# Two edits of VectorE's instruction order in a fused attention and expert layer: the block choice ahead of the key marks, two expert passes ahead of the selected normalization

## The reference

```python
s_b = einsum('bhtd,bhnd->bhtn', q, k_c) / scale
logits_c = where(c_ok, s_b, NEG)
_, top_idx = top_k(logits_c, 4)                       # the block choice
...
logits_s = where(allowed, einsum('bhtd,bhtnd->bhtn', q, k_s) / scale, NEG)
out_s = einsum('bhtn,bhtnd->bhtd', softmax(logits_s), v_s)
...
sc, ix = top_k(sim, 8)                                # key scores
scores, pk = top_k(all_sc, 8)                         # pair sums
w = silu(einsum('btd,bthkd->bthk', h, de)) * softmax(scores)
experts_states = einsum('bthk,bthkd->btd', w, ue)
```

## Time and profile before

| | |
|---|---|
| median of 3 runs | 1492.84 us (1491.62 to 1496.29) |
| profiled execution | 1490.08 us |
| its span, first to last instruction | 1488.3 us |
| mean granted TensorE clock | 0.981 |
| busy | PE 1399.5, PEld 1041.1, DVE 1148.8, ACT 927.1, POOL 946.8 us |
| the 1152.1 us from 252.1 on (30 units) | PE 1128.6, DVE 985.2, ACT 759.6, POOL 792.2 us busy, clock 1.00 |

### The profile page before, as it was taken

The page is one execution under the profiler, slowest core; times in us unless marked ns, Lnnn a source line. Parts: engine busy times, 40 slices in busy tenths (PEclk is TensorE's granted clock), DMA queues, the critical chain, the costliest instruction groups (busy, mean ns, idle before and its releaser), DMA issues. The chain is left out here.

```text
span 1488.3 us, 43616 instructions
## 1 busy us (share of the span) xinstructions
PE 1399.5 (94%) x14864; PEld 1041.1 (70%) x14960; DVE 1148.8 (77%) x4512; ACT 927.1 (62%) x1684; POOL 946.8 (64%) x877
## 2 busy tenths in 40 slices
PE   6899569999999999999999999999999999999978
PEld 4566437777777777777777777777777777777757
DVE  5444378888888888888888888888888888888712
ACT  3776436666666666666666666666666666666641
POOL 4655357777777766666666666666676666666720
PEclk8999969999999999999999999999999999999989
DMA  6556842211112222222212222122222222222027
GB/s 187 202 192 213 269 82 54 52 44 48 46 47 51 52 52 52 52 50 47 47 47 47 50 52 47 48 52 52 52 52 52 52 52 52 66 52 53 9 83 250
DMA packets 217149, 113.76 MB, mean 76 GB/s; under 512 B 128872, under 2 KB 211224, under 8 KB 217112
## 3 DMA queue, kind: packets, MB, share of 16 engines
q1 hardware_dynamic: 216304, 112.88, 27.9%
q10 hardware_dynamic: 808, 0.42, 0.2%
HBM read 73.08 MB, written 40.16 MB: 76 GB/s over the span
## 5 line engine op out<-in xcount | busy, mean ns | idle before, releaser
L1394 DVE TENSOR_REDUCE bmax<-q_bank 128x32 f32<-128x512 f32 (+3 forms) x512 | 221.2, 487 | 34.4 <-PE q_bank L1635 34.2
L1149 POOL TENSOR_TENSOR sumxy<-xy 128x1024 f32<-128x1024 f32 x128 | 246.1, 1942 | 0.0
L1241 ACT ACTIVATE pts<-k_bank 128x512 f32<-128x512 f32 (+2 forms) x384 | 177.4, 490 | 42.2 <-PE k_bank L1670 41.4
L1115 POOL TENSOR_TENSOR pad<-pad 128x1 f32<-128x1 f32 x32 | 6.2, 193 | 287.4 <-DVE top L1413 287.4
L1495 DVE SCALAR_TENSOR_TENSOR mw<-sumxy,c,ex 128x1024 f32<-128x1024 f32 x128 | 162.0, 1287 | 13.4 <-ACT ex L1259 9.6
L1617 PE MATMUL f_bank<-xt,wfu 128*128 128x128 f32 x1024 | 162.4, 281 | 0.0
L1635 PE MATMUL q_bank<-ko,qo 96*128 96x512 bf16 (+3 forms) x512 | 142.6, 306 | 16.9 <-DVE bmax L1394 16.7
L1175 POOL TENSOR_TENSOR cw<-cw,mw 128x1024 f32<-128x1024 f32 x64 | 150.9, 2358 | 11.5 <-ACT mw L1265 8.9
L1617 PE MATMUL f_bank<-xt,wfg 128*128 128x128 f32 x1024 | 150.3, 279 | 0.0
L1617 PEld LDWEIGHTS f_bank<-xt,wfu 128*128 128x128 f32 x1024 | 139.4, 191 | 11.5
L1318 ACT ACTIVATE oT<-k_bank 128x512 f32<-128x512 f32 x64 | 38.2, 597 | 173.8 <-PE k_bank L1685 129.3
(11 more groups left out here) (211 smaller groups left out, 3307.8 us busy)
## 6 DMA issues: line engine op xcount, KB each, us to landing
qo<-s_qs SPq DMA_DIRECT2D x192, 64.0 KB, 2.2
ko<-s_ks SPq DMA_DIRECT2D x186, 64.0 KB, 2.2
s_qs<-parts SPq DMA_DIRECT2D x8, 768.0 KB, 4.7
s_ks<-parts SPq DMA_DIRECT2D x8, 768.0 KB, 6.3
s_v<-vo SPq DMA_DIRECT2D x8, 544.0 KB, 3.0
vv<-s_v SPq DMA_DIRECT2D x32, 136.0 KB, 2.3
vw<-s_v SPq DMA_DIRECT2D x64, 68.0 KB, 2.5
xin<-in_L_attn_x_dram SPq DMA_DIRECT2D x8, 512.0 KB, 7.1
```

Source lines behind the costliest of these rows:

```text
L1149: done("sum_done", g_.tensor_tensor(sumxy[:, h, :, :], xy[:, 0, h, 0:XK, None].broadcast_to([P, XK, KEYS]), xy[:, 1, h, None, :].broadcast ...
L1241: last = s.activation(pts[:, h, OFFS[j]:OFFS[j] + n], bank[:, 0:n], ACT.Exp)
L1394: last = v.tensor_reduce(bmax[:, i, h, 0:n], Q.bank(job)[:, o:o + n * BLK].rearrange("p (n j) -> p n j", j=BLK), AX.X, ALU.max)
```

## The change

In VectorE's step `unselected(n, now=t)` moves from behind head 2's block maxima to a place ahead of `key_marks(n)`. `expert(., 0)` and `expert(., 1)` move from the start of the step of their own unit to the end of the step ahead, behind `pair_sums` and ahead of `normalize(t, 0)`; `lead` gets them for unit 0. No instruction is added or dropped, and no other engine's program changes.

```diff
@@ lead(n), VectorE
                     local_scores(n)
                     selected_max(n)
                     cn.end()
+                    expert(n, 0)
+                    expert(n, 1)
 
                 def step(t):
                     n = None if t.tail else t.next()
                     cf.start(t)
-                    expert(t, 0)
-                    expert(t, 1)
                     expert_silu(t, 0)
                     expert(t, 2)
                     expert_silu(t, 1)
@@ step(t)
                     expert_sum(t)
                     if n:
+                        unselected(n, now=t)
                         key_marks(n)
                     gate(t, 1)
                     if n:
                         for part in range(3):
                             block_max(n, 2, part)
                     if n:
-                        unselected(n, now=t)
                         best_pairs(n)
                     up(t, 1)
```

## The result

The changed kernel takes 1512.61 us (median of 6 runs, 1509.89 to 1514.29), the kernel before 1492.08 us (6 runs). The ratio is 1.0132, with a 95% interval of 1.0116 to 1.0148. The prediction was 1507 us with a range of 1500 to 1519.

What follows compares the result with a forecast made beforehand. TensorE, busy 94% of the span, and its waits for VectorE were taken as the bound. 0.46 us in 31 steps gave 14.3 us, the passes 0: 1490.1 + 14.3 = 1504.4 profiled, 1507 us median with 2.8 added; range 1500 to 1519.

Steps and rivals of the forecast that it cites:

- TensorE and VectorE in step between the loads of head 1 and head 2: From 730.2 to 734.5 in a unit: VectorE is the later engine, TensorE waits microsecond for microsecond for anything added.
- The choice costs 0.43 us in its new place: Block choice straight behind expert_sum: 0.43 us instead of 1.97, as GpSimd's third sum has ended by then.
- The chained wait costs 0.04 us, 0.46 in all: Marks wait for the choice's end: 0.04 us, making 0.46 us a unit with the choice, 14.3 us over 31 steps.
- its high end: Pause behind the choice of 0.15 us, as at 737.48, instead of 0.04: 0.58 us a unit.
- the nearer row: Rows of the same form with GpSimd idle, the lead's and the marks' link, taken as grounds for 0.46 us.
- the marks' link: Chained wait between the marks' last replace and xy, 0.04 us, taken as the model for the choice's.
- The lead's row: The choice's instruction in the lead, where GpSimd stands idle: 0.43 us, taken for its new place.
- The freed time at the old place is worth nothing: Behind head 2's maxima VectorE gains some 2.1 us, which becomes idle time because TensorE itself is late next.
- The passes meet `shift_s` and `at` and take turns with them: Tail: pass 0 waits for shift_s, ends 750.67; at follows to 751.40; pass 1 ends 752.48.
- cover of 0.6 us: Tail: VectorE stands ready for pass 2 at 754.7, which is due at 755.32.
- The earlier front gains nothing, pass 2 hangs on ScalarE: Front of a unit: 2.48 us without passes turn idle, pass 2 stays at 755.32 behind ScalarE's exponential; gain 0.
- The lead costs nothing: Lead, which gets the passes for unit 0: the prediction's sum has no term for it.

Runs made afterwards that it cites:

- e1: From the kernel before, only the block choice moves ahead of the key marks; the expert passes stay. 1511.09 us, ratio 1.0129.
- e3: From the kernel before, only the choice moves, with the key marks' own wait for the best keys put ahead of it. 1506.95 us, ratio 1.0091.
- e5: As e1, with the choice's instruction issued a second time ahead of it into a tile that nothing reads. 1519.31 us, ratio 1.0183.
- e2: From the kernel before, only the two expert passes move into the tail; the block choice stays. 1495.01 us, ratio 1.0011.
- e7: e6 with the two expert passes moved into the tail, as in the changed kernel. 1480.95 us, ratio 0.9925.
- e8: As e2, but in the lead the passes wait until GpSimd has finished pc. 1492.84 us, ratio 1.0005.
- e6: From the kernel before, second half of the strike-outs behind head 2's maxima, block choice behind the second up product. 1477.05 us, ratio 0.9902.
- e4: From the kernel before, second half of the strike-outs moves behind head 2's maxima, straight ahead of the block choice. 1487.93 us, ratio 0.9975.

## Why the prediction was right, point by point

- *TensorE and VectorE in step between the loads of head 1 and head 2; what is put there is paid in full.* Right. e1 (0.58 us a unit), e3 (0.10 less) and e5 (0.33 more) move in the unit's length what they move on VectorE, to 0.02 us.
- *The choice costs 0.43 us in its new place, with no GpSimd instruction against it.* Right: 0.41 us. GpSimd's small instruction starts 0.31 us behind the running sum (744.83), before 0.32, and doesn't get ahead.
- *The chained wait costs 0.04 us, 0.46 in all.* This term was mis-sized. It is 0.15 us, which the prediction had seen at 737.48 and kept as its high end: 0.58 us a unit (its own terms give 0.57), which is what was measured. The reason for the nearer row was wrong: the marks' link is followed by no second wait, the choice's is, and in a loop that wait's value is computed in a register. e3 and the written-out unit show it. With 31 units this accounts for 3.7 of the 5.6 us by which 1507 was too low. The lead's row, with constant waits, was no guide to the loop.
- *The freed time at the old place is worth nothing.* Right: VectorE's waits for query products went from 34.2 to 99.2 us.
- *The passes meet `shift_s` and `at` and take turns with them; pass 0 ends 1.08 us behind `shift_s`; cover of 0.6 us.* Right to 0.15 us for the turns: `shift_s` ended at 763.50, pass 0 at 764.57, `at` at 765.16, pass 1 at 766.24. The cover was larger, 0.91 us: the result ended 3.91 us behind `shift_s` (767.41), worked out were 4.24. Pass 2 was also due 0.11 us later against `shift_s`, and 0.13 us of the gain went into the wait for the tanh. The same tanh makes one reading of the prediction wrong: without the meeting its rows give a cover of 0.95 us, not of 2, because the silu half waits for 753.69 in any case. These rows agree with the rule that the prediction cites from the Trainium skill, "SBUF — State Buffer", section "Who interferes with whom", on a VectorE instruction with two SBUF inputs.
- *The earlier front gains nothing, pass 2 hangs on ScalarE.* Right: e2's units, and e7's where TensorE no longer waits for VectorE.
- *The lead costs nothing.* This was not priced, and the same rule would have told it. In the lead pass 0 gets its turn ahead of `pc`, and TensorE starts on `pc` 1.0 us later against the start of the unit (e8 undoes it). It is at most 1 us, and in e2 the first unit is longer by 0.1.

The sum: 0.58 us in each of the 31 units that prepare another one is 18.0 us of the 20.5 between the medians; the other 2.5 us are not placed. The profiled executions differ by 24.2 us: 17.4 in units 1 to 30, 2.3 us in the first unit, 4.2 us before it, 0.3 behind.

The 2.3 us of the first unit can be told apart. The choice is 0.56 of them, as e1's first unit has 42.60 us. The rest fits a second stretch at half clock that only this execution has. In all ten profiles the granted TensorE clock is 0.50 when the first unit begins and 1.00 from 1.7 to 4.4 us later on. In that of the changed kernel it then goes back once more, to 0.50 from 220.69 to 224.10. In the 3.41 us at 1.00 ahead of that TensorE was busy for 1.34 us, as it waited 2.07 us for `pc`; in e2 and e7 a wait of 1.75 us had no such fall behind it. The two stretches (us, PE, PEld, DVE, ACT and POOL busy, granted clock, DMA share, GB/s):

```profile
217.28:220.69 3.41, 1.34 (x6) 0.69 (x6) 3.38 (x5) 1.08 (x3) 3.33 (x4) 1.00 0.01 2
220.69:224.10 3.41, 3.41 (x7) 1.36 (x6) 1.93 (x3) 2.00 (x4) 0.93 (x1) 0.50 0.00 0
```

TensorE is busy throughout the second, and 3.41 us at half the clock are worth at most 1.7 us (an estimate).

The 4.2 us before the first unit are not the passes' doing. The first unit began at 214.1 to 215.4 us in the profiles of the three kernels with the passes in the lead and no wait ahead (changed, e2, e7), and at 210.1 to 212.4 in the seven others. But TensorE's first product of the lead, which lies ahead of everything that was moved, already starts at 191.4 to 192.7 us in those three and at 187.7 to 189.7 in the others. The time from there to the first unit is 22.1 to 22.7 us in all ten. Why the stages ahead of it ended later in these three is open; no run here separates it from scatter. It would account for e7's 3.9 and e2's 2.5 us.

## What to carry to other kernels

Before moving an instruction, find the two waits of the bound engine between which its new place lies: there it is paid in full, elsewhere it may be free, and 0.4 us without a wait can cost more than 2 us spent waiting where nobody is late. An engine's idle time is a place for work only up to the next thing that it must deliver: e6 moved 1.4 us of the same engine's work across the last such point and gained nearly what both waits were worth (0.50 of 0.57 us a unit). A price taken from a lead or a written-out step doesn't hold in the loop if waits follow each other there.

## What the runs showed of the hardware

- Behind the choice, a second wait on a value that the loop computes costs 0.11 us straight behind a chained one (pause 0.15 against 0.04 us), while with constant waits it is not seen. Moving it ahead of the chained instruction hides it (e3). The price is not the same at every place: between the strike-outs and the choice e4 has 0.04 us in one half of the loop and 0.25 in the other.
- An instruction of 0.4 us that needs GpSimd's turn can cost 0.52 or 2.15 us, decided by 0.04 us: it gets its turn at the boundary between two GpSimd instructions, and only if it stands ready then (e4). In the tail both engines' long instructions then alternate; neither waited for more than one instruction of the other (changed kernel, 762.48 to 766.24).
